# Feed-forward output products with a 512-column weight operand, and a tile-by-tile residual

## The reference, cut to what matters

```
for i in range(6):
    h = gelu(x @ W1[i].T + B1[i])           # 256 -> 1024
    x = h @ W2[i].T + B2[i] + x             # 1024 -> 256, and the residual
    if i < 5:
        x = layernorm(x) * LN_G[i] + LN_B[i]
```

## Time and profile before

| | before |
|---|---|
| median of 3 runs | 1099.56 us (1096.92 to 1102.39) |
| profiled execution | 1097.38 us, span 1095.6 us, 1.8 us around it |
| PE busy | 1008.1 us (92%) |
| PEld busy | 836.9 us (76%) |
| DVE busy | 745.4 us (68%) |
| ACT busy | 611.1 us (56%) |
| POOL busy | 370.6 us (34%) |
| chain that ended last | PE 54%, of it line 1846 24% and line 1829 24%; DVE 6%, ACT 3% |
| granted TensorE clock, mean | 0.961 of 2.4 GHz |

### The profile page before, as it was taken

How to read it: one execution, slowest core, us unless ns; L and a number is a source line. 1 busy time by engine, 2 the same in 40 slices (tenths; PEclk the granted TensorE clock), 3 DMA queues, 4 the chain that set the end, 5 groups by cost and what they waited for, 6 DMA issues and landing times.

```text
span 1095.6 us, 18205 instructions
## 1 busy us (share of the span) xinstructions
PE 1008.1 (92%) x6589; PEld 836.9 (76%) x6589; DVE 745.4 (68%) x2033; ACT 611.1 (56%) x1176; POOL 370.6 (34%) x714
## 2 busy tenths in 40 slices
PE   6788998989989788788999999999999999999996
PEld 5455554555747788577899998999999899999995
DVE  4676685867638668756757667776667777677746
ACT  4466566665258555645755456665556665466640
POOL 3444355462131444525633222224222233222600
PEclk9599898998999989999999999999999999999998
DMA  7000000013020001012010010110101011010111
GB/s 240 21 2 20 3 20 20 22 32 105 27 76 3 1 2 39 1 77 65 33 58 30 11 39 1 39 34 6 40 1 39 1 39 40 1 39 1 39 40 39
DMA packets 29234, 36.91 MB, mean 34 GB/s; under 512 B 1780, under 2 KB 26584, under 8 KB 29144
## 3 DMA queue, kind: packets, MB, share of 16 engines
q1 hardware_dynamic: 24600, 31.02, 8.7%
q10 hardware_dynamic: 4544, 4.72, 1.4%
HBM read 31.40 MB, written 4.20 MB: 32 GB/s over the span
## 4 chain that ended last, share of the span: by engine, by line
PE 54%; DVE 6%; ACT 3%; POOL 2%; issue 1%; DMA 1%; SPq 0%; DVEq 0%; POOLq 0%; ACTq 0%
PE ps L1846 24%; PE ps L1829 24%; PE ps L1801 2%; PE ps L1719 1%; ACT xn L1968 1%; DVE xT_l L2223 1%; DVE ln_stats L2205 1%; PE ps L1770 1%; PE ps L1672 1%; DMA mlp_b<-L_ffn_LN_B 1%; DVE ln_stats L86 1%; ACT hs L1968 0%; POOL x_b L1620 0%; PE ps L1733 0%; ACT x_b L1984 0%
## 5 line engine op out<-in xcount | busy, mean ns | idle before, releaser
L2062 ACT ACTIVATE G<-ps,bias_col 128x512 f32<-128x512 f32 x192 | 136.0, 708 | 185.7 <-PE ps L1829 176.5
L1846 PE MATMUL ps<-w_h,G_h 128*128 128x256 f32 x736 | 208.2, 283 | 0.0
L1846 PE MATMUL ps<-w_h,G_l 128*128 128x256 f32 x736 | 207.9, 282 | 0.0
L1846 PE MATMUL ps<-w_l,G_h 128*128 128x256 f32 x736 | 207.8, 282 | 0.0
L2330 DVE TENSOR_TENSOR G_l<-G,G_h 128x512 fp32r<-128x512 f32 x192 | 155.3, 816 | 60.0 <-ACT G_h L2063 60.0
L1648 POOL TENSOR_TENSOR x_a<-xn,mlp_g 128x1024 f32<-128x1024 f32 x20 | 67.6, 3378 | 344.8 <-DVE xn L2360 344.8
L681 ACT ACTIVATE probs<-ps 128x512 f32<-128x512 f32 (+3 forms) x256 | 98.6, 442 | 111.8 <-PE ps L817 111.6
L1829 PE MATMUL ps<-xT_h,w_h 128*128 128x512 f32 x384 | 152.0, 396 | 1.0 <-issue 1.0
L1065 DVE CUSTOM_DVE_ANT_0 ps<-ps,q_mask 128x128 f32<-128x128 f32 (+3 forms) x256 | 120.8, 512 | 44.6 <-PE ps L806 43.2
L1829 PE MATMUL ps<-xT_h,w_l 128*128 128x512 f32 x384 | 150.6, 392 | 0.0
L1829 PE MATMUL ps<-xT_l,w_h 128*128 128x512 f32 x384 | 150.4, 392 | 0.0
(11 more groups left out here) (299 smaller groups left out, 2117.1 us busy)
## 6 DMA issues: line engine op xcount, KB each, us to landing
w_raw<-L_ffn_W_T SPq DMA_DIRECT2D x12, 1024.0 KB, 5.3
hs<-L_attn_hidden_states SPq DMA_DIRECT2D x8, 512.0 KB, 4.1
x_kept<-hs SPq DMA_DIRECT2D x4, 512.0 KB, 3.1
w_raw<-x_kept SPq DMA_DIRECT2D x2, 1024.0 KB, 5.5
out<-xn SPq DMA_DIRECT2D x3, 512.0 KB, 2.9
w_raw<-L_ffn_ent_w_T SPq DMA_DIRECT2D x1, 1024.0 KB, 10.0
w_raw<-L_ffn_ent_pw SPq DMA_DIRECT2D x1, 1024.0 KB, 12.5
heads_T<-neg_rows SPq DMA_DIRECT2D x64, 2.0 KB
```

The lines of the kernel that those rows point to most:

```text
L1846: mm = pe.matmul(ps[:, 4 + t // 2, (t % 2) * D:(t % 2 + 1) * D], x[b % 2][f][:, t * P:(t + 1) * P], w2_chunk(w, f), start=(k == 0), stop=( ...
L2062: act.activation(G32[n % 4], bank, ACT.Gelu, bias=bias)
```

## The change

The high and low parts of a W2 chunk are stored next to each other, `w2_hl[f // 2][:, f % 2, 0 or 1, :]`, so that both together are one operand of 512 columns. `output` now issues two matmuls for each chunk: G_h with both parts (512 columns), which fills a whole bank with the high product on the left and the low product on the right, and G_l with the high part (256 columns), which is summed into the left half. A tile needs a whole bank for this, so the four tiles of a turn take banks 4, 5, 4, 5, and a tile waits until VectorE has read the tile two before it (`v_tile`). `residual` adds tile by tile, in two dependent instructions of 128x256 for each: left half plus `x_a`, then right half plus that.

```diff
-    w2_h = [put(nc, f"w2_h{n}", g.heads, n * 2 * D, [2, D], F32R) for n in range(4)]
-    w2_l = [put(nc, f"w2_l{n}", g.probs, at * 2 * D, [2, D], F32R) for n, at in enumerate((2, 3, 6, 7))]
+    w2_hl = [put(nc, f"w2_hl{n}", place, at * D, [2, 2, D], F32R) for n, (place, at) in
+             enumerate(((g.heads, 0), (g.heads, 4), (g.probs, 4), (g.probs, 12)))]
+    w2_h, w2_l = ([both[:, :, n, :] for both in w2_hl] for n in range(2))
...
+    def tile_of(i, b, t):
+        return RT * (turn_of(i, b) - 1) + t
...
         def output(i, b):
             pe.wait_ge(feed["v_gl"], i * HB + (b + 1) * FC)
             if b == 0:
                 pe.wait_ge(feed["v_w"], i * 8 + 4)
-            if i or b:
-                pe.wait_ge(feed["v_sum"], turn_of(i, b) - 1)
-            else:
-                pe.wait_ge(second["v_sum"], B)
             for t in range(RT):
-                k = 0
+                n = tile_of(i, b, t)
+                if n >= 2:
+                    pe.wait_ge(feed["v_tile"], n - 1)
+                elif n == 0:
+                    pe.wait_ge(second["v_sum"], B)
+                tokens = slice(t * P, (t + 1) * P)
                 for f in range(FC):
-                    for x, w in ((G_h, w2_h), (G_h, w2_l), (G_l, w2_h)):
-                        mm = pe.matmul(ps[:, 4 + t // 2, (t % 2) * D:(t % 2 + 1) * D],
-                                       x[b % 2][f][:, t * P:(t + 1) * P], w2_chunk(w, f),
-                                       start=(k == 0), stop=(k == 3 * FC - 1))
-                        k += 1
-            mm.then_inc(feed["p_out"], 1)
+                    parts = [(G_h, ps[:, 4 + t % 2, :], w2_hl[f // 2][:, f % 2, :, :].rearrange("p a d -> p (a d)")),
+                             (G_l, ps[:, 4 + t % 2, 0:D], w2_chunk(w2_h, f))]
+                    for k, (x, bank, w) in enumerate(parts if f < FC - 1 else parts[::-1]):
+                        mm = pe.matmul(bank, x[b % 2][f][:, tokens], w, start=(f == 0 and k == 0),
+                                       stop=(f == FC - 1 and k == 1))
+                mm.then_inc(feed["p_tile"], 1)
...
         def residual(i, b):
-            v.wait_ge(feed["p_out"], turn_of(i, b))
+            v.wait_ge(feed["p_tile"], tile_of(i, b, 0) + 1)
...
-            v.tensor_tensor(g.rsum[:, :, :], ps[:, 4:6, :].rearrange("p a (b c) -> p (a b) c", c=D),
-                            g.x_a[:, b * RT:(b + 1) * RT, :], ALU.add).then_inc(feed["v_sum"], 1)
+            for t in range(RT):
+                n = tile_of(i, b, t)
+                v.wait_ge(feed["p_tile"], n + 1)
+                row = g.rsum[:, t, :]
+                chain.step(v.tensor_tensor(row, ps[:, 4 + t % 2, 0:D], g.x_a[:, b * RT + t, :], ALU.add))
+                chain.settle()
+                v.tensor_tensor(row, ps[:, 4 + t % 2, D:2 * D], row, ALU.add).then_inc(feed["v_tile"], 1)
```

More of the change, by code:

```diff
@@ L233, in build @@
                         "p_proj v_sum g_whole g_xa x3_out0 x3_out1 p_T a_xh v_xl a_w1 v_w1", "second_")
-        g.feed = sems(top, nc, "p_T a_T v_T a_w v_w p_hid a_g v_gl p_out v_sum v_norm g_mul g_res g_bb "
+        g.feed = sems(top, nc, "p_T a_T v_T a_w v_w p_hid a_g v_gl p_tile v_tile v_norm g_mul g_res g_bb "
                       "x3_in0 x3_in1 y_out0 y_out1 g_x3 p_last v_y", "feed_")
@@ L2022, in weight_high @@
                 if i:
-                    act.wait_ge(feed["p_out"], i * B)
+                    act.wait_ge(feed["p_tile"], RT * i * B)
                 else:
@@ L2059, in gelu @@
             if f == 0 and (turn_of(i, b) > 2):
-                act.wait_ge(feed["p_out"], turn_of(i, b) - 2)
+                act.wait_ge(feed["p_tile"], RT * (turn_of(i, b) - 2))
             bank = ps[:, hidden_bank(i, n), :]
@@ L2343, in residual @@
                 v.wait_ge(feed["v_norm"], turn_of(i, b) - 1)
-            v.tensor_tensor(g.rsum[:, :, :], ps[:, 4:6, :].rearrange("p a (b c) -> p (a b) c", c=D),
-                            g.x_a[:, b * RT:(b + 1) * RT, :], ALU.add).then_inc(feed["v_sum"], 1)
+            for t in range(RT):
[5 more added lines that the diff above has]
+                v.tensor_tensor(row, ps[:, 4 + t % 2, D:2 * D], row, ALU.add).then_inc(feed["v_tile"], 1)
         def norm(i, b, last):
-            v.wait_ge(feed["v_sum"], turn_of(i, b))
+            v.wait_ge(feed["v_tile"], tile_of(i, b, RT))
             steps = rstd_steps(v, chain, g.lnw, [g.rsum[:, k, :] for k in range(RT)], g.lnw["y"][:, :])
```

## The result

| | before | after |
|---|---|---|
| median of 4 runs | 1099.8 us | 1189.2 us (1186.7 to 1194.6) |
| ratio, 95% interval | 1 | 1.082 (1.078 to 1.085) |
| profiled execution | 1097.4 us, span 1095.6 | 1186.7 us, span 1184.9 |
| PE busy, of the span | 92% | 88% |
| mean granted clock | 0.961 | 0.931 |

The change makes the kernel 8% slower. The forecast was 1177 us, in a range of 1143 to 1207.

A forecast was written before the change was run, and what follows sets the result against it. TensorE alone was taken to bound the kernel from 535 us on. The sum was 1097.4 + 55.3 (waits, with the product gain) - 0.35 (last chain) + 24 (clock) = 1176 us, 1177 as a median; range 1143 to 1207.

The forecast's parts named there:

- Products: In each output, one 512- and one 256-column matmul per chunk replace three of 256: 6.6 us gained over 23 turns.
- VectorE's place in the queue, 6.65 - g: Tile 2 waits for VectorE: a turn changes by 6.65 us minus VectorE's old idle time before `residual` (g); 55.3 us summed.
- The two adds of a tile: VectorE's two dependent 128x256 adds of a tile take 0.88 us before TensorE can go on.
- GpSimd beside the adds: In b = 0 turns, adds beside GpSimd's `x_a` instruction cost 0, at most one 2.7 us instruction in 5 turns.
- rival D: VectorE arrives earlier, as half clock gives ScalarE time and `x_a` no longer covers `low_next`: 25 us go, 1152; chance 0.14.
- The x3 add in turn (5,0): Tile 0's adds wait for GpSimd's x3 add, 11.4 us after this output's start: +6.5 us.
- VectorE's last chain: After output (5,2), VectorE is free 0.35 us sooner, where its last chain begins: -0.35 us.
- The clock: TensorE's granted clock falls to 0.50 after most new stalls: 27 us, less 3 for engines catching up; bounds 0 and 58.
- Rival A: The same TensorE stalls, but the granted clock stays at 1.00: 1152, 1154 as a median; chance 0.17.
- Rival B: TensorE never waits, VectorE reads tile 0 within 5.57 us every turn, only the matmul gain stands: 1093; chance 0.04.
- C: Half clock begets stalls: it falls after most stalls, for two stretches each, 58 us in place of 24: 1211; chance 0.10.

The follow-up runs named there:

- the kernel with the idle matmuls: The changed kernel with 512-column matmuls that nobody reads put ahead of tile 2's wait, to fill the stall: 1157.4 us, ratio 1.051.
- the products alone: The changed kernel without the wait for the tile before last, VectorE adding once at the end as before: 1091.5 us, ratio 0.992 against the kernel before.
- The turned order: The changed kernel with VectorE's adds of tiles 0 and 1 ahead of `low_next`: 1101.0 us, ratio 1.002 against the kernel before.
- the wait alone: The changed kernel with three 256-column products again and one add a tile, banks and wait kept: 1164.8 us, ratio 1.058 against the kernel before.
- the two kernels with one add a tile: The wait alone (1164.8 us), and the changed kernel with the right half's add left out (1163.1 us, ratio 1.060 against the kernel before).

## Why the prediction was right, by its own steps

- **Products** (-6.6 us): right, measured -5.8. A chunk takes 11.11 / 32 = 347 to 11.28 / 32 = 352 ns, 348 was taken.
- **VectorE's place in the queue, 6.65 - g**: right to 0.2 us in a turn of blocks 1 to 4, to 0.3 in turn (5,0). In the kernel with the idle matmuls, where the clock held, the outputs of blocks 1 to 4 grew by 1.97, 2.91, 3.33 and 2.90 us for b = 0 to 3 and turn (5,0) by 6.77; 1.82, 2.84, 3.21, 2.83 and 6.5 were forecast. Over the 23 outputs that is 57.7 us (321.3 - 263.6) for 55.3. The stalls forecast (2.2, 3.1, 3.5, 3.1 and 6.9) are what a turn takes over the products alone; the idle time that the profile shows is 0.2 to 0.3 us less (1.95, 2.86, 3.30, 2.86 and 6.62), since a stall costs more than its idle time. That VectorE's lateness renews itself each turn held as well: stall after stall is the same. The turned order shows that the place in the queue is needed for the loss, the wait alone that the new products are not.
- **The two adds of a tile** (0.88 us before TensorE is let go): right; one of them left out shortened each stall by 0.46.
- **GpSimd beside the adds** (0): right, the adds took 0.42 us, also in turn (5,0), where GpSimd works beside them. GpSimd beside `low_next` was named in rival D only as something that might vanish; it didn't, but it is the other half of what makes the stall. Its cost was in the g of the rows, and so in the sum.
- **The x3 add in turn (5,0)**: right, VectorE waited 4.58 us for it.
- **VectorE's last chain** (-0.35 us): right. From the first matmul after output(5, 2) to the end of the span it took 22.35 us before and 22.00 after.
- **The clock** (24 us): mechanism right, term too small. It is 32 by the idle matmuls. I took 14 falls after the stalls of about 3 us at 1.5 us each; there were 14, but three of them lasted 6.8 us and cost 2.6 each, 24.4 in all instead of 21. I took half of the four after b = 0; all four came, 6.0 instead of 3. The long stall's fall cost 1.5 instead of 3. And I took 3 us off because a hidden at half clock would let ScalarE and VectorE catch up: no hidden ran at half clock, every slow stretch ended inside its output, so that term had nothing behind it.

The profiled execution took 1186.7 us, where the sum said 1176: 8 of the 10 us are the clock, 2 the wait. In the clock term one error, the fall of turn (5,0) taken 1.5 us too dear, hid a part of the others.

Rival A (the clock holds) fell: all 19 stalls of 1.95 us and more in the profiled execution were followed by 0.50. The idle matmuls show what the kernel would take with the clock held, 1157; A had 1154. Rival B had no turn for it but the three that were named. C, two stretches after every fall, came true for 4 of 19. D's condition never came up, since no hidden was slowed; no stall got shorter in later turns.

## What to carry to other kernels

When a wait for a reader is put into the middle of a stream that had none, look up when the reader's queue gets there: the idle time that it now has in front of its instruction, against the point at which the new code needs it, gave the cost of the wait here to 0.3 us a turn before anything was built. An engine that is 67% busy can still be 3 us late every turn: the new products are worth 5.8 us, and the place of a few lines in VectorE's order decided whether they came with 88 us of loss. In this kernel a stall of TensorE cost its idle time, 0.3 us more, and 1.5 us for a slow stretch of 3.4 us behind it.

## What the runs showed that I had not expected

The clock turns small changes of a stall into large ones: stalls 0.46 us shorter were worth 9 us as waiting and 24 us in all. Of 38 stalls over 1 us in the two kernels with one add a tile, 8 of 8 at 1.35 to 1.49 us left the clock at 1.00, 6 of 18 at 2.27 to 2.41 us, and none of the 12 longer ones; in the changed kernel all four of 1.95 us were followed by 0.50. So the length of a stall alone does not decide; what else does, no run here shows. Matmuls whose results nobody reads, put into the wait, gave 32 us back.
